# Expert weights loaded from another queue, two slots ahead, and a new order of the work between attention and feed-forward

## What is computed

```python
x = x + tanh(g_xattn) * attention(layernorm(x), ctx, ctx, mask)   # 8 sequences of 112x256, ctx 375x256, 16 heads of 16
y = layernorm(x)
w = softmax(tanh(mean(y) @ W1 + b1) @ W2 + b2)     # per sequence: 8 zones, the best 3 kept and renormalised
x = x + tanh(g_ffn) * (y + sum of w[e] * (gelu(y @ Wa[e]) @ Wb[e]))   # Wa 256x1024, Wb 1024x256
```

## Time and profile before

| what | value |
|---|---|
| runs of before | 347.06, 348.01, 348.06 us, median 348.01 |
| profiled execution | 344.57 us, its span 342.5 us |
| PE busy in the span | 294.1 us (86%) |
| PE weight loads | 243.5 us (71%) |
| DVE / ACT / POOL busy | 202.3 / 195.2 / 159.4 us |
| TensorE clock, mean over the span | 0.975 of full |
| weights' DMA | 32 of 512 KB, from POOL's queue |

### The profile page before, as it was taken

How to read it: one execution, slowest core, us unless ns; L and a number is a source line. 1 busy time by engine, 2 the same in 40 slices (tenths; PEclk the granted TensorE clock), 3 DMA queues, 4 the chain that set the end, 5 groups by cost and what they waited for, 6 DMA issues and landing times.

```text
span 342.5 us, 9360 instructions
## 1 busy us (share of the span) xinstructions
PE 294.1 (86%) x3348; PEld 243.5 (71%) x3348; DVE 202.3 (59%) x617; ACT 195.2 (57%) x406; POOL 159.4 (47%) x217
## 2 busy tenths in 40 slices
PE   1819679799999989989979855798899999999996
PEld 1415457577676766767756535798899999999996
DVE  7226857476687776867676331655555664456452
ACT  3223666777767767777776863453466345445432
POOL 3725896859978699786989872001000000000000
PEclk9967999999999999999999996999999999999999
DMA  6953877857767687674764340100100101001000
GB/s 160 299 145 109 225 203 176 220 166 194 220 161 231 174 220 211 168 223 120 219 154 142 82 138 0 42 3 22 48 23 21 42 3 43 26 20 42 2 15 15
DMA packets 33180, 40.53 MB, mean 118 GB/s; under 512 B 10248, under 2 KB 26944, under 8 KB 33136
## 3 DMA queue, kind: packets, MB, share of 16 engines
q1 hardware_dynamic: 26416, 22.16, 24.6%
q0 software_dynamic: 4784, 16.98, 16.6%
q10 hardware_dynamic: 1936, 0.79, 0.9%
HBM read 33.09 MB, written 6.74 MB: 116 GB/s over the span
## 4 chain that ended last, share of the span: by engine, by line
PE 56%; DMA 13%; POOL 10%; ACT 7%; issue 6%; DVE 3%; SPq 2%; DVEq 1%; ACTq 0%; POOLq 0%
PE bank L1219 16%; PE bank L1238 16%; PE bank L1064 7%; DMA k_scr<-wb 4%; DMA qbd<-q_scr 4%; POOL wb L460 3%; DMA stage<-in_L_ffn_Wb 3%; PE bank L1014 3%; POOL wa L460 3%; POOL stage L455 2%; PE bank L1026 2%; PE bank L1073 2%; PE bank L1046 2%; PE bank L1030 2%; ACT pT L545 2%
## 5 line engine op out<-in xcount | busy, mean ns | idle before, releaser
L769 DVE CUSTOM_DVE_ANT_0 bank<-bank,maskb 112x375 f32<-112x375 f32 x128 | 67.9, 571 | 44.2 <-PE bank L1014 44.1
L1219 PE MATMUL bank<-ctxT,wqkvo 128*128 128x112 f16 x960 | 61.4, 216 | 10.9 <-DVE qbd L944 10.9
L1219 PEld LDWEIGHTS bank<-ctxT,wqkvo 128*128 128x128 f16 x960 | 59.0, 100 | 12.5 <-issue 12.1
L1238 PE MATMUL bank<-wb,stage 128*112 x576 | 66.8, 273 | 0.0
L1238 PEld LDWEIGHTS bank<-wb,stage 128*112 128x112 f16 x576 | 62.3, 130 | 0.2
L732 ACT ACTIVATE kst<-bank 128x448 f32<-128x448 f32 x48 | 25.7, 535 | 57.1 <-PE bank L1219 57.0
L545 ACT ACTIVATE pT<-bank 125x448 f32<-125x448 f32 x96 | 48.7, 539 | 7.1 <-PE bank L1030 6.4
L943 DVE COPY wqkvo<-wa 128x3072 f16 x24 | 23.2, 966 | 42.7 <-PE bank L1219 38.2
L1014 PE MATMUL bank<-kst,qbd 128*112 128x375 f16 x128 | 33.2, 334 | 16.5 <-DMA qbd<-q_scr 13.3
L455 POOL TENSOR_SCALAR stage<-stage 128x512 f32<-128x512 f32 x64 | 39.6, 631 | 13.1 <-DMA stage<-in_L_ffn_Wb 6.4
L460 POOL TENSOR_TENSOR wa<-stage,wa 128x512 f16<-128x512 f32 x32 | 37.0, 1167 | 12.9 <-ACT wa L655 12.3
(11 more groups left out here) (125 smaller groups left out, 449.6 us busy)
## 6 DMA issues: line engine op xcount, KB each, us to landing
stage<-in_L_ffn_Wa POOLq DMA_DIRECT2D x16, 512.0 KB, 4.4
stage<-in_L_ffn_Wb POOLq DMA_DIRECT2D x16, 512.0 KB, 5.2
kst<-k_scr SPq DMA_DIRECT2D x64, 93.8 KB, 3.6
k_scr<-wb SPq DMA_DIRECT2D x16, 187.5 KB
ctx_s<-in_ctx SPq DMA_DIRECT2D x8, 336.0 KB
qbd<-q_scr SPq DMA_DIRECT2D x32, 56.0 KB, 3.7
xa<-in_x SPq DMA_DIRECT2D x8, 112.0 KB, 4.3
q_scr<-wb SPq DMA_DIRECT2D x16, 56.0 KB, 3.2
```

The lines of the kernel that those rows point to most:

```text
L769: v.tensor_tensor_reduce(out=bank[0:SQ, e, 0:SK], in0=bank[0:SQ, e, 0:SK], in1=maskb[0:SQ, b % 2, 0:SK], scale=-1.0, scalar=FLOOR, op0=ALU ...
L1219: ins = T.matmul(o, first(ws, t, f), x2b[:, b % 2, (xs * DT + t) * SQ:(xs * DT + t + 1) * SQ], start=(t == 0 and xs == 0 and ws == 0), sto ...
L1238: ins = T.matmul(o, hT[:, u % 2, hs * FT * SQ + f * SQ:hs * FT * SQ + (f + 1) * SQ], wb[:, bass.ds(e * (4 * CHUNK) + ws * (2 * CHUNK) + f ...
```

## The change

The weights' loads move from POOL's block to SP's, at four places of each iteration, and each is issued two slots ahead of the slot that handles its parts. The parts start two slots later (slot 2 of iteration -1), two in every slot, and end in slot 1 of iteration 7. DVE's copy_weights(0) moves into iteration 7, ahead of residual(6). TAIL gets a new order and new units, with the pieces of ACT and DVE moved to suit; ACT's hidden(0) goes ahead of normed2(6).

```diff
@@ parts_at
-            n = min(2 if i < 0 or j < 3 else 1, NPART - at)
+            n = min(2 if (i, j) >= (-1, 2) else 0, NPART - at)
@@
-TAIL = (("X2T", B - 2), ("OT", B - 1), ("ON", B - 1), ("OP", B - 1), ("X2T", B - 1), ("H", 1), ("L", 1), ("W", 1))
+TAIL = {0: ("OT", B - 1), 1: ("X2T", B - 2), 2: ("ON", B - 1), 3: ("OP", B - 1), 5: ("X2T", B - 1), 7: ("H", 1), 8: ("L", 1), 11: ("W", 1)}
@@ SP
+            def load_parts(b, slot):
+                for k in parts_at(b + (slot + 2) // 4, (slot + 2) % 4)[::2]:
+                    z, q = k // PARTS, k % PARTS
+                    i = k % RING
+                    need(sp, s["lo_done"], k - RING + 2)
...
                 move_max(b, 1)
+                load_parts(b, 0)
                 load_xr(o)
                 load_ctx(m + 1)
                 load_x(m + 1)
                 load_mask(m)
+                load_parts(b, 1)
                 write_k(m, 0)
                 write_k(m, 1)
                 write_q(m)
                 move_max(n, 0)
+                load_parts(b, 2)
...
                 read_k(m, 0)
                 read_q(m, 0)
+                load_parts(b, 3)
                 store_r(b - 2)
@@ POOL
-            for k in range(0, RING, 2):
-                load_parts(k)
...
                     for k in ks:
                         lo_part(k)
-                        if k % 2:
-                            load_parts(k + RING - 1)
@@ ACT
             o_copy(B - 1)
-            normed2(B - 2)
             act.wait_ge(s["lo_done"], NPART)
             hidden(0)
+            normed2(B - 2)
             for u in range(B * TOPK):
                 if u + 1 < B * TOPK:
                     hidden(u + 1)
-                if u == 0:
+                if u == 1:
                     x2_hi(B - 2)
                 if u == 2:
                     ot_copy(B - 1)
-                if u == 3:
+                if u == 4:
                     normed2(B - 1)
-                if u == 4:
+                if u == 5:
                     x2_hi(B - 1)
-                if u == 5:
+                if u == 7:
                     route_hidden(1)
-                if u == 6:
+                if u == 9:
                     route_exp(1)
@@ DVE, iteration loop
                 split_max(n, 1)
+                if b == B - 1:
+                    dve.wait_ge(s["idx_loaded"], 16)
+                    dve.wait_ge(s["hi_done"], NPART)
+                    dve.wait_ge(s["lo_done"], NPART)
+                    full(dve, ("V1", B - 1))
+                    dve.wait_ge(s["pe_st"], tile(B - 1, 0, 0))
+                    copy_weights(0)
                 residual(o)
@@ DVE, units
                 low(u)
                 if u == 0:
+                    o_rows(B - 1)
                     result(B - 2)
+                if u == 2:
                     x2_lo(B - 2)
-                if u == 1:
-                    o_rows(B - 1)
-                if u == 3:
+                if u == 4:
                     residual(B - 1)
-                if u == 4:
+                if u == 5:
                     result(B - 1)
+                if u == 6:
                     x2_lo(B - 1)
-                if u == 6:
+                if u == 9:
                     route_logits(1)
-                if u == 7:
+                if u == 10:
                     route_top(1)
-                if u == 8:
+                if u == 12:
                     route_shares(1)
@@ PE
             g1(0)
+            put(TAIL[0])
...
-                if u < 7:
+                if u > 0 and u in TAIL:
                     put(TAIL[u])
-                if u == 8:
-                    put(TAIL[7])
```

More of the change, by code:

```diff
@@ L97, in __init__ @@
                     names.append(name)
-        for i, name in enumerate(TAIL):
+        for i, name in enumerate(TAIL.values()):
             names.append(name)
@@ L349, in move_max @@
                                  ms[:, h, :, :].rearrange("r g q -> r (g q)")).then_inc(rq_in[h], 16)
+            def load_parts(b, slot):
[3 more added lines that the diff above has]
+                    need(sp, s["lo_done"], k - RING + 2)
+                    dst = stage[:, i:i + 2, :]
+                    if q < 4:
+                        sp.dma_start(dst.rearrange("p a f -> p (a f)"),
+                                     Wa[z, (q // 2) * 128:(q // 2) * 128 + 128, :]).then_inc(part_loaded[i // 2], 16)
+                    else:
+                        sp.dma_start(dst.rearrange("p a (f n) -> p (a f) n", n=D),
+                                     Wb[z, (q - 4) * 256:(q - 2) * 256, :].rearrange("(f p) n -> p f n", p=128)).then_inc(part_loaded[i // 2], 16)
             def load_xr(b):
@@ L435, in _ @@
             chain = Steps(pool, s["pool_chain"])
[L437 to L449, removed]
             def scale_part(k):
@@ L886, in route_shares, with copy_weights @@
                 v.tensor_copy(wbc[:, b0 * TOPK:(b0 + n) * TOPK], spare_bank(("W", g))[:, 0:n * TOPK]).then_inc(s["wbc_done"], 1)
+            def copy_weights(u):
+                if u == ROUTES[1][0] * TOPK:
+                    dve.wait_ge(s["idx_loaded"], 32)
+                e = dve.value_load(idx_row[0:1, u:u + 1], min_val=0, max_val=NZ - 1)
+                need(dve, s["g1_done"], 2 * u)
+                v.tensor_copy(wst3, wa[:, bass.ds(e * (4 * CHUNK), 3 * CHUNK)]).then_inc(s["wst_done"], 1)
+                v.tensor_copy(wst1, wa[:, bass.ds(e * (4 * CHUNK) + 3 * CHUNK, CHUNK)]).then_inc(s["wst_done"], 1)
             v.memset(qbd[:].rearrange("p a e j f -> p (a e j f)"), 0.0).then_inc(s["zeroed"], 1)
@@ L935, in _ @@
                     route_shares(0)
[L937 to L944, removed]
             def low(u):
@@ L959, in put_out @@
                                        op0=ALU.mult, op1=ALU.add).then_inc(s["y_done"], 1)
[L961 to L966, removed]
             for u in range(B * TOPK):
```

## The result

The changed kernel takes 330.56 us in the median (328.42 to 331.40), against 347.53 us for the kernel before in the same comparison: ratio 0.9586, 95% interval 0.9526 to 0.9645. The direction and most of the steps at the border held; the step on attention had the wrong sign. The profiled execution took 328.42 us, its span 326.3 us, so in spans the gain is 16.2 us. A repeat in another set of runs gave 330.88 us. Executions of one kernel fall into a faster state and a slower one; the ratios, and the medians of the experiments, are of the faster ones alone, but the profiles of the border's order and of the extra load are of slower ones.

A forecast was written before the change was run, and what follows sets the result against it. PE was taken to bound attention nearly and the feed-forward wholly, with the loss at the border. A and B 7.8, C 2.2, D 1.9, E -2.0 sum to 9.9, about 10 us: 348.01 to 338.0 us, range 333 to 345.

The forecast's parts named there:

- A: Border: weights ready before attention ends, so the index comes next and g1(0) starts earlier; 5.9 us gained alone.
- B: Attention's iterations 6 and 7: idle time of PE cut by 1.1 and 1.5 us, starting g1(0) earlier.
- C: g1(0) at the border: with under 2 us of idle time it runs at 2.4 GHz, gaining 2.2 us.
- D: Border order: stalls before g1(1), g1(2), g1(5), g1(6) shrink or go, a new one before g1(12) costs 0.8; net 1.9 us.
- E: Attention: loads on SP ahead of the reads cost 0.6 us a read; some 2 us lost, between -1 and +16.
- F: The rest: POOL's time falls to about 15.5 us an iteration, ACT's grows 0.6, both hidden behind PE; 0, bound 2 us.
- Rival 4: Attention: POOL's freed time takes 0.4 us of idle time off each iteration and E is nothing; 333 us, chance 0.05.
- Rivals 1: Attention: reads somewhat later, 1 to 1.5 us each instead of 0.6, 8 us lost; 344 us, chance 0.17.
- rival 2: Attention: the load ahead of the reads is paid in full, 2.3 us for each of seven; 352 us, chance 0.09.
- Rival 3: Border: weights still come last and end the wait, leaving a gain of 3 to 5 us; 344 us, chance 0.07.

The follow-up runs named there:

- the extra load: Changed kernel with POOL's 1/sigma ahead of the scaling, plus one more 512 KB DMA ahead of the load of slot 2 in iterations -1 to 5: 342.69 us.
- 1/sigma first: Changed kernel with POOL's layernorm 1/sigma ahead of the scaling of the next parts in slots 0 and 3: 329.55 us.
- the second experiment: Kernel before with only the new TAIL order and its pieces on ACT and DVE: 343.19 us against 345.07, ratio 0.9926.

## Why the prediction was right or wrong, step by step

In the profiled execution A and B gave 6.1 us for the 7.8 forecast, C 2.1 for 2.2, D 3.4 for 1.9, and E plus 2.4 for minus 2.0. For the 2.2 us before iteration 2 no step had a term.

**A, right.** The weights no longer end the wait, the index comes next, at 192.81 plus 0.76. Undoing the slots costs 5.4 us, the early copy 2.9; the two overlap, so they don't add up.

**B, wrong.** I took 2.6 us off iterations 6 and 7; they lost 0.2 together. Iteration 6 had 1.8 us idle instead of my 1.3. In iteration 7, I reckoned with the work taken off ACT. But PE's waits for ACT's exponentials stayed (1.7 us, 1.8 before), ACT itself waiting 1.1 us for POOL's 1/sigma of the second layernorm, 0.8 before. I also overlooked that W(0) in slot 2 is the end of a serial chain (ACT's exponential, nine steps on DVE): the wait for it grew from 0.4 to 1.04 us. With 1/sigma first, PE's waits for the exponentials fell to 0.5 and that for W(0) grew to 1.7; moving W(0) and the exponential as well made iteration 7 as short as step B had it. That g1(0) began at 198.6 and not 201.5 is in spite of B, and 1.9 us of it is the early start that the repeat lacks: there g1(0) began at 202.1.

**C, right.** g1(0) took 2.52 us at a clock of 1.00, 2.1 less than 4.63. The 2.36 that I subtracted is a g1's share of the chain; from start to end it takes 2.52.

**D, right, its size short.** 3.4 us instead of 1.9 (my 0.4, 0.2 and 2.0 make 2.6, not 2.7). The stalls before g1(2), g1(5) and g1(6) all went. The new one before g1(12) exists: 0.24 us here and 1.87 in the second experiment, against 0.8 taken.

**E, the step that failed.** "Net +0.6 us a read ... some 2 us lost". The price of the load was sized well (0.38 of issue for 0.5, landing median 3.1 for 3.4), but I read PE's slot 0 as bound by the reads, because landing and need lay within 0.2 us of each other. ACT, waiting 6.9 us in four iterations for POOL's 1/sigma, held slot 0 as well, and I did not list it. The change sped that up, so iterations 2 to 5 gained 2.4 us (1.2 in the repeat) where I had them lose.

**F, wrong in its weight.** POOL's time was "hidden behind PE". Its busy time was (16.0 to 16.1 us an iteration, I had said 15.5), but a 0.6 us operation inside POOL's order was not. That the same operation moved ahead of the scaling gives 3.4 to 3.7 us in the kernel before shows it.

**The rivals.** Rival 4, "attention gains too", with a chance of 0.05, is the one that came about, for the reason I gave it, POOL's freed time, and on top of the forecast's border: PE's idle time in iterations 2 to 5 fell from 4.7 to 3.4 us, 0.3 an iteration. I had not seen that the place of 1/sigma was what made it count. Rivals 1 and 2 did not come about; a second load ahead costs somewhat less than rival 2's price. Rival 3 did not.

## What to carry to other kernels

When two engines wait at the same place, the smaller slack in the trace does not say which of them binds: list every wait that ends there, the short ones of helper engines too, and ask where the operation waited for stands in its engine's queue. A tiny result that others wait for belongs ahead of bulk work that waits for transfers; here that order alone was worth some 3.5 us. Taking work off an engine before a serial chain of small steps may only move the wait, unless the step that needs the chain's end moves too.

## What the runs showed that I had not expected

A DMA of 512 KB costs SP 0.40 us to issue in the median for `Wb`, half of POOL's 0.84, and 0.41 for `Wa`, where POOL took 0.61; from SP it lands in 4.3 to 4.4 us in the median. One such load ahead of six dependent reads cost PE nothing measurable in iterations 2 and 3, the second 1.5 to 1.9 us a time. The Trainium skill's page "DMA: Bandwidth & Descriptors", section "Issuing engines are not separate DMA queues", says that issuing from several engines saves only the sequencer's time, usually small next to the DMA; here the issuer was worth 10.7 us, and 6.3 with 1/sigma first. Some 4 of the 10.7 thus hang on POOL's order, in which a result that ACT waits for stood behind the loads and their landing; the rest is open.

TensorE's clock: g1(0) took 2.52 us after 0.4 us of idle time, 3.98 after 4.0, 4.35 after 4.9 and 4.63 after 6.3. The granted clock of these four stretches was 1.00, 0.60, 0.55 and 0.50 of 2.4 GHz, so the last ran at 1.2 GHz throughout.
